# Third group of the first layer as four quadrant matmuls, with the conv stream and its turning moved around the inverses

## The chip, the cores and the metric

The kernel runs on one core of one Trainium2 chip. The time is device microseconds of that core from start to end of one execution, as the median of several runs.

## The reference

The input is an image batch of 4 x 48 x 128 x 128 (fp32). Two residual parts follow each other:

```python
x = x + conv_ref(ln_c(x))      # layer norm over channels; 3x3 conv on 12 of the 48 channels;
                               # 1x1 conv 48 -> 254; rfft2 on 8x8 patches, times fft_w, irfft2;
                               # gelu(a) * b on the two halves of 127; 1x1 conv 127 -> 48
t = tokens(x)
t = t + ffn_ref(ln_t(t))       # 48 -> 192 -> 48 with relu; inputs and weights rounded to fp8 e5m2,
x = from_tokens(t)             # sums and activations rounded to fp16
```

The first layer of the second part has 192 outputs: two times 128 rows hold the first 128 of them, and 64 are left. They are called the third group here.

## The kernel before

The work is cut into 32 steps, each a band of 16 image rows (two half bands j of 8 rows, 48 channels each, at partitions 0 and 64). It is a pipeline over seven steps: in step t the x of band t is transposed, the conv of band t-2 is made, the mix (1x1 conv) and the patch transforms of band t-3 and the end of those of t-4, the first layer of band t-5 and the second layer of band t-6. `live(t, d)` says whether band t-d exists, `at(t, d)` is its number. The loops run t = 0 to 34 (`run`), then comes a drain written out by hand. The program is unrolled. Every engine has its own `step(t)` with a hand-written order, and the engines meet by semaphores only, so an engine's order of work and its waits set the schedule. There is no planner.

What TensorE does in a step (lines 761 to 883): transposes of x into banks 0 and 1 (L784), the forward transform or coefficients (L803), inverse 3 of the band before (L532 its first half, L539 its second), mixes 0 and 1 (L519), projection (L548), second layer (L632, L639), inverse 0, turn of the tokens (L653), turn of the row statistics (`rows`, L613), turn of the rest (L663), mix 2. Then comes the part that is changed: first layer groups 0 and 1 of half c = 0 (`hidden`, L619), first half of inverse 1, group 2 of c = 0 (in `last_group`), second half of inverse 1, the conv `stream` (L568) into bank 3, mix 3, groups 0, 1 and 2 of c = 1, the turning of the conv (`convolve`, L577, from the copy `convs` back into bank 3), inverse 2. In steps 3 to 5 the row statistics are turned in `last_group`, from step 6 on earlier in the step, behind the turn of the tokens.

Groups 0 and 1 use 48 rows each (0 to 47 and 64 to 111) and all 128 columns, one per half band. Group 2 uses both half bands at once: rows 0 to 111, with weights `l1h[:, 2]` that are block diagonal. Each group's 512 columns are the tokens of half c. ScalarE copies them to `hid16` (`accumulators`, L897), VectorE adds the bias and cuts at zero (`relu`, L1276), and one step later ScalarE converts to `hid8` (`activations`, L906) for `second_layer`.

Other operations that are spoken of: ScalarE's gelu (L889) behind the first half of each inverse, its copy of the stream to `convs` (L1114) and its read of the turned conv into `zpix` (L1122, semaphore `conv_read`), `rows` (L913, the copy of the turned statistics to `rm_t`), and `convert` in the drain (L985). VectorE's `gate` (L1245), `weigh` (L1234) and `low_parts` (L1222, `zl`). The row statistics go from `rm_t` by SP's DMAs to `rm_scratch` (L403) and back to `crm` (L415), GpSimd makes the normalised conv channels from them (L1513 to L1521), SP stores these (L308) and loads the nine shifted `taps` (L333, L335), which the stream reads.

Steps with t below 8 or from 24 on are called peeled. In them TensorE waits at the top for everything of the step before:

```python
before = lambda behind: min(t[1] - behind, STEPS)
...
pe.wait_ge(conv_read, upto(before(2)))
...
pe.wait_ge(hid16_ready, upto(6 * before(5)))
```

In the others `conv_read` is waited for only ahead of the coefficients (L803).

## Time and profile before

| | us |
|---|---|
| runs | 699.67, 699.83, 700.46 |
| median of the runs | 699.83 |
| span of the profiled execution | 699.4 |

| engine | busy us | share |
|---|---|---|
| TensorE (PE) | 666.5 | 95% |
| its weight loads (PEld) | 529.3 | 76% |
| VectorE (DVE) | 597.9 | 85% |
| ScalarE (ACT) | 536.8 | 77% |
| GpSimd (POOL) | 456.9 | 65% |

All durations in the prediction are of the profiled execution; no own total besides its span is given for it. A busy share of 95% is an average over filling, steps and drain. Matmuls are pipelined: a matmul of 128 columns is shown with 0.27 us and the next starts 0.11 us later, so the start of one group and the start of the next say how long TensorE's array is taken.

### The profile page before, as it was taken

What the parts mean: (1) busy time and instruction counts of PE and PEld (TensorE: products, weight loads), DVE (VectorE), ACT (ScalarE), POOL (GpSimd) and SP (SyncE); (2) the same over time, 40 slices, a digit from 0 to 9 for tenths busy, and PEclk for the clock granted to TensorE, in tenths of its full rate; (3) what the DMA queues carried; (4) which work ended last, traced back from release to release, by engine and by line L of the source; (5) the groups of instructions that cost most, each with busy time, mean ns of one, the idle gap of its engine ahead of it and who ended that gap; (6) DMA issues with size and microseconds to landing.
All of it is one profiled execution on the core that took longest, in us unless ns stands there. A gap on an engine that the chain in (4) does not pass through costs nothing.

```text
span 699.4 us, 19176 instructions
## 1 busy us (share of the span) xinstructions
PE 666.5 (95%) x6620; PEld 529.3 (76%) x6620; DVE 597.9 (85%) x1159; ACT 536.8 (77%) x1087; POOL 456.9 (65%) x347
## 2 busy tenths in 40 slices
PE   4879999999999999999999999999999999999984
PEld 4657877778778877787878877787788777887751
DVE  7637889988988899988988899889888999877877
ACT  4244568888888888888889888888888888877784
POOL 2605677767777777677776877677777876753353
PEclk9989999999999999999999999999999999999995
DMA  4434445444544554445444544545445543342102
GB/s 102 79 78 118 121 113 131 112 126 128 142 120 118 142 140 121 114 120 138 127 123 131 139 131 107 132 121 144 121 116 144 139 129 103 100 119 87 47 23 68
DMA packets 52207, 80.73 MB, mean 115 GB/s; under 512 B 20823, under 2 KB 36079, under 8 KB 52111
## 3 DMA queue, kind: packets, MB, share of 16 engines
q1 hardware_dynamic: 50031, 78.56, 43.2%
q10 hardware_dynamic: 2080, 0.94, 0.6%
q8 instruction: 54, 0.88, 0.6%
q14 instruction: 42, 0.34, 0.2%
HBM read 63.17 MB, written 16.30 MB: 114 GB/s over the span
## 4 chain that ended last, share of the span: by engine, by line
PE 87%; DVE 3%; DMA 3%; issue 2%; ACT 1%; SPq 1%; POOL 1%; DVEq 0%; ACTq 0%; POOLq 0%
PE inva L532 17%; PE invb L539 15%; PE mixp L519 13%; PE misc L548 8%; PE misc L803 8%; PE misc L619 4%; PE misc L519 4%; PE misc L663 3%; PE misc L784 3%; PE misc L568 2%; PE misc L577 2%; PE misc L653 2%; PE mixp L632 2%; PE mixp L639 2%; DMA xin<-in_x_dram 1%
## 5 line engine op out<-in xcount | busy, mean ns | idle before, releaser
L1555 POOL TENSOR_TENSOR st<-st,neg_half 128x16 f32<-128x16 f32 x32 | 93.3, 2915 | 129.2 <-DVE st L1459 129.2
L532 PEld LDWEIGHTS inva<-inv,gmix 128*127 128x127 f32 x1024 | 123.4, 191 | 25.3 <-issue 16.6
L532 PE MATMUL inva<-inv,gmix 128*127 128x128 f32 x1024 | 141.0, 281 | 0.6 <-DVE gmix L1234 0.6
L1234 DVE TENSOR_TENSOR gmix<-mixp,freq_w 128x508 f32<-128x508 f32 x192 | 122.6, 680 | 16.9 <-PE mixp L519 16.9
L539 PE MATMUL invb<-inv,gmix 128*127 128x128 f32 x1024 | 134.7, 274 | 0.1
L539 PEld LDWEIGHTS invb<-inv,gmix 128*127 128x127 f32 x1024 | 126.2, 191 | 2.1 <-DVE hbuf L1245 0.5
L897 ACT ACTIVATE hid<-misc 128x512 f16<-128x512 f32 x180 | 94.1, 599 | 17.7 <-PE misc L619 17.7
L1245 DVE TENSOR_TENSOR hbuf<-gact,invb 127x512 f32<-127x512 f32 x128 | 87.4, 683 | 22.2 <-ACT gact L889 17.7
L1584 POOL TENSOR_TENSOR st<-st,neg_half 128x16 f32<-128x16 f32 x31 | 95.4, 3077 | 16.4 <-DVE st L1313 15.9
L906 ACT ACTIVATE hid<-hid 128x512 fp8e5<-128x512 f16 x174 | 93.2, 619 | 0.0
L889 ACT ACTIVATE gact<-inva 127x512 f32<-127x512 f32 x128 | 77.5, 605 | 19.9 <-PE inva L532 19.3
L519 PE MATMUL mixp<-win,zh 60*128 60x254 f16 x768 | 89.9, 272 | 0.7 <-DVE gmix L1234 0.6
L519 PE MATMUL mixp<-win,zl 60*128 60x254 f16 x768 | 89.0, 267 | 0.0
L1538 POOL TENSOR_TENSOR ob<-tch,y 112x1024 f32<-112x1024 f32 x29 | 62.1, 2140 | 34.1 <-DVE y L1294 34.1
L977 ACT ACTIVATE y<-mixp 112x512 f16<-112x512 f32 x58 | 31.4, 594 | 47.0 <-PE mixp L639 47.0
L803 PE MATMUL misc<-fwd,zpix 128*124 128x128 f32 x512 | 62.1, 275 | 0.0
L548 PE MATMUL misc<-hbuf,wout 127*64 127x512 f32 x248 | 60.1, 605 | 0.0
L803 PEld LDWEIGHTS misc<-fwd,zpix 128*124 128x124 f32 x512 | 58.6, 188 | 0.0
L519 PEld LDWEIGHTS mixp<-win,zh 60*128 60x128 f16 x768 | 37.1, 93 | 26.8 <-issue 14.5
L1435 DVE TENSOR_REDUCE st<-xpix 128x16 f32<-128x768 f32 x32 | 30.5, 952 | 28.3 <-ACT xpix L1068 28.3
L1580 POOL TENSOR_TENSOR tcen<-tpix,st 128x768 f32<-128x768 f32 x31 | 45.7, 1475 | 12.5 <-DVE st L1301 9.6
L1068 ACT ACTIVATE xpix<-misc 128x384 f32<-128x384 f32 x64 | 31.6, 494 | 23.2 <-PE misc L784 22.1
(184 smaller groups left out, 1358.2 us busy)
## 6 DMA issues: line engine op xcount, KB each, us to landing
taps<-cz_scratch SPq DMA_DIRECT2D x63, 292.2 KB
xin<-in_x_dram SPq DMA_DIRECT2D x64, 192.0 KB, 3.3
xres<-in_x_dram SPq DMA_DIRECT2D x64, 192.0 KB, 4.1
out_dram<-ob SPq DMA_DIRECT2D x60, 192.0 KB, 2.6
taps<-cz_scratch SPq DMA_DIRECT2D x63, 146.1 KB
crm<-rm_scratch SPq DMA_DIRECT2D x58, 96.0 KB
cx<-in_x_dram SPq DMA_DIRECT2D x32, 96.0 KB
cz_scratch<-cz SPq DMA_DIRECT2D x63, 48.8 KB
```

The costliest lines, as they stand in the source:

```text
L519: mm = pe.matmul(pair[q][:, e * HID2:(e + 1) * HID2], zpart[r0:r0 + KC, 2 * s + e, :], win[r0:r0 + KC, wpart, :], start=(e == 0 and zpart ...
L532: mm = pe.matmul(inva[0:HID, q * PX:(q + 1) * PX], gmix[:, s % 2, q, 0:HID], inv[:], start=True, stop=True, skip_group_check=True)
L539: mm = pe.matmul(invb[0:HID, q * PX:(q + 1) * PX], gmix[:, s % 2, q, HID:HID2], inv[:], start=True, stop=True, skip_group_check=True)
L548: mm = pe.matmul(dst[HALF * j:HALF * j + HALF, :], wout[:], hbuf[:, half, j, :, :], start=True, stop=True, skip_group_check=True)
L803: mm = pe.matmul(bank[(3, 0)[i // 4]][0:KSPAN, (i % 4) * PX:(i % 4 + 1) * PX], zpix[:, ring(t, 3), i, 0:KSPAN], fwd[:], start=True, stop=True,
L889: act.activation(gact[:, s % 2], inva[0:HID, :], ACT.Gelu).then_inc(gelu_ready, 1)
L897: act.activation(hid16[:, 3 * c + g, :], bank[g][:], ACT.Copy).then_inc(hid16_ready, 1)
L906: act.activation(hid8[:, 3 * c + g, :], hid16[:, 3 * c + g, :], ACT.Copy, saturate=False)\
L1234: dve.tensor_tensor(gmix[:, s % 2, 2 * q:2 * q + 2, 0:HID2], pair[q][:, 0:2 * HID2].rearrange("p (e c) -> p e c", e=2), freq_w[:], ALU.mul ...
L1245: dve.tensor_tensor(hbuf[:, s // 2, :, 2 * e:2 * e + 2, :], gact[:, s % 2].rearrange("p (j i c) -> p j i c", j=2, i=2), invb[0:HID, :].rea ...
L1555: pool.tensor_tensor(st1[:, 6, :], st1[:, 5, :], neg_half[:], ALU.pow).then_inc(pow1, 1)
L1584: pool.tensor_tensor(st2[:, 6, :], st2[:, 5, :], neg_half[:], ALU.pow).then_inc(pow2, 1)
```

## The change

Group 2 of both halves is made by `hidden_rest`: four matmuls of 48 rows by 64 columns, one for each pair of half band j and token half c. Half band j takes rows from 64 j on, token half c takes output partitions from 64 c on, and the result of half band j lies in bank 2 + j with both token halves one above the other. `hid16` and `hid8` have a new order of slots: 0 and 1 for c = 0, 2 (j = 1) and 3 (j = 0) for the rest, 4 and 5 for c = 1. The second layer reads slots 3 and 2 in `rest_product`, with as many matmuls as before.

TensorE's order from mix 2 on is now: groups 0 and 1 of c = 0, inverse 1 whole, `hidden_rest`, the row statistics (steps 3 to 5), mix 3, groups 0 and 1 of c = 1, stream, first half of inverse 2, the turning of the conv, second half of inverse 2. ScalarE's order is: copies 0 and 1, gelu 1, copies 2 and 3, rows (steps 3 to 5), copy 4, `convs`, copy 5, gelu 2, read of the conv. VectorE has three bias operations of two slots each. New waits: the stream and the early row statistics on copy 2, the second half of the transposes of x on copy 5 (in the steps that aren't peeled), `hidden_rest` on both squares `tsq`. In step 2 stream and turning stay together. In the drain the order of slots is followed, and the second layer inside inverse 3 waits for four conversions.

```diff
--- before.py
+++ after.py
@@ -560,6 +560,8 @@
                     pe.wait_ge(lo_ready, upto(2 * n + 2))
                 if live(t, 0):
                     pe.wait_ge(rmT_ready, a + 1 if a > 2 else 1)
+                if live(t, 5):
+                    pe.wait_ge(hid16_ready, 6 * at(t, 5) + 3)
                 pe.wait_ge(col_in, upto(64 * (c + 1)))
                 for turn in range(2):
                     rows = taps[:, turn].rearrange("p (r w) -> p r w", w=PW)
@@ -609,15 +611,34 @@
                 else:
                     pe.wait_ge(gmix_ready, upto(8 * n + 2))
                     pe.wait_ge(y16_ready, upto(2 * at(t, 6) + 2))
+                if live(t, 5) and a < ROWS_EARLY:
+                    pe.wait_ge(hid16_ready, 6 * at(t, 5) + 3)
                 dst = bank[3] if a < ROWS_EARLY else mixp[0]
                 pe.transpose(dst[0:32, 0:128], rm[:].rearrange("p a j i -> p (a j i)"), eye[:])\
                   .then_inc(rmT_done, 1)
 
+            def hidden_rest(t):
+
+                for c in range(2):
+                    for j in (1, 0):
+                        r0 = HALF * j
+                        mm = pe.matmul(bank[2 + j][HALF * c:HALF * c + HALF, :], l1h[r0:r0 + CH, 2, r0:r0 + HALF],
+                                       q16[r0:r0 + CH, 4 * c:4 * c + 4, :], start=True, stop=True,
+                                       skip_group_check=True)
+                        if c == 1:
+                            mm.then_inc(hid_done, 1)
+
             def hidden(t, c, g, dst):
 
                 r0, r1 = ((0, CH), (HALF, SPAN), (0, SPAN))[g]
                 pe.matmul(dst[:], l1h[r0:r1, g, :], q16[r0:r1, 4 * c:4 * c + 4, :], start=True, stop=True,
                           skip_group_check=True).then_inc(hid_done, 1)
+
+            def rest_product(dst, c, j):
+
+                r0, o = HALF * c, HALF * j
+                return pe.matmul(dst[o:o + HALF, :], l2[:, 2, r0:r0 + HALF], hid8[:, (3, 2)[j], :],
+                                 start=False, stop=True, skip_group_check=True)
 
             def second_layer(t):
 
@@ -627,17 +648,16 @@
                 pe.wait_ge(hid8_ready, upto(6 * l + 5))
                 pe.sem_inc(pe_held, 1)
                 for c in range(2):
-                    for g in range(2):
-                        r0 = HALF * g
-                        pe.matmul(pair[c][r0:r0 + HALF, :], l2[:, g, r0:r0 + HALF], hid8[:, 3 * c + g, :],
-                                  start=True, stop=False, skip_group_check=True)
-                for c in range(2):
                     if c == 1:
                         pe.wait_ge(hid8_ready, upto(6 * l + 6))
                         pe.sem_inc(pe_held, 1)
-                    for r0 in (0, HALF):
-                        mm = pe.matmul(pair[c][r0:r0 + HALF, :], l2[:, 2, r0:r0 + HALF], hid8[:, 3 * c + 2, :],
-                                       start=False, stop=True, skip_group_check=True)
+                    for g in range(2):
+                        r0 = HALF * g
+                        pe.matmul(pair[c][r0:r0 + HALF, :], l2[:, g, r0:r0 + HALF], hid8[:, 4 * c + g, :],
+                                  start=True, stop=False, skip_group_check=True)
+                for c in range(2):
+                    for j in range(2):
+                        mm = rest_product(pair[c], c, j)
                     mm.then_inc(y_done, 1)
 
             def turn_tokens(t):
@@ -691,6 +711,15 @@
                     for g in range(3):
                         hidden(t, c, g, dst[g])
 
+                def older_half(c, dst):
+                    for g in range(2):
+                        r0 = HALF * g
+                        pe.matmul(dst[r0:r0 + HALF, :], l2[:, g, r0:r0 + HALF], hid8[:, 4 * c + g, :],
+                                  start=True, stop=False, skip_group_check=True)
+                    for j in range(2):
+                        mm = rest_product(dst, c, j)
+                    mm.then_inc(y_done, 1)
+
                 def second_layer_half(c, dst):
                     for g in range(2):
                         r0 = HALF * g
@@ -704,11 +733,12 @@
                 t = (0, DRAIN)
                 pe.wait_ge(lo_ready, 2 * STEPS)
                 pe.wait_ge(h_ready, 4 * NEW + 2)
+                pe.wait_ge(hid16_ready, 6 * OLDER + 3)
                 project_half(0, bank[3])
 
                 def between():
-                    pe.wait_ge(hid8_ready, 6 * OLDER + 3)
-                    second_layer_half(0, mixp[0])
+                    pe.wait_ge(hid8_ready, 6 * OLDER + 4)
+                    older_half(0, mixp[0])
 
                 inverse(t, 4, 3, between)
                 pe.wait_ge(hid16_ready, 6 * OLD)
@@ -720,7 +750,7 @@
                 project_half(1, mixp[1])
                 pe.wait_ge(hid8_ready, 6 * OLD)
                 pe.wait_ge(y16_ready, 2 * OLDER + 1)
-                second_layer_half(1, mixp[0])
+                older_half(1, mixp[0])
                 pe.wait_ge(tpix_ready, 2 * NEW + 1)
                 pe.wait_ge(tsq_ready, 2 * NEW + 1)
                 first_layer(OLD, 0, (bank[0], bank[2], invb))
@@ -781,6 +811,8 @@
                         pe.wait_ge(eye_in, 16)
                     pe.wait_ge(xord_ready, upto(a + 1))
                     for i in range(PAIRS):
+                        if i == 4 and not peeled:
+                            pe.wait_ge(hid16_ready, upto(6 * l + 6))
                         mm = pe.transpose(bank[i // 4][:, (i % 4) * 128:(i % 4) * 128 + XSPAN],
                                           xord[:, i * PX:(i + 1) * PX], eye[0:XSPAN, 0:XSPAN])
                         if i % 4 == 3:
@@ -844,37 +876,29 @@
                     hidden(t, 0, 0, bank[0])
                     hidden(t, 0, 1, bank[1])
 
-                def last_group():
-                    if live(t, 0) and 3 <= a < ROWS_EARLY:
-                        rows(t, 0)
-                    if live(t, 5):
-                        pe.wait_ge(tsq_ready, upto(2 * m + 1, 2 * STEPS))
-                        hidden(t, 0, 2, bank[2])
-
-                if live(t, 3):
-                    inverse(t, 3, 1, last_group)
-                else:
-                    last_group()
+                if live(t, 3):
+                    inverse(t, 3, 1)
+                if live(t, 5):
+                    pe.wait_ge(tsq_ready, upto(2 * m + 2, 2 * STEPS))
+                    hidden_rest(t)
+                if live(t, 0) and 3 <= a < ROWS_EARLY:
+                    rows(t, 0)
                 if a == 2:
                     keep_busy(16, bank[1])
-                if live(t, 2):
-                    stream(t)
-                    if peeled and a == 2:
-                        keep_busy(2, bank[1])
                 if live(t, 3):
                     mix(t, 3)
                 if live(t, 5):
                     pe.wait_ge(hid16_ready, upto(6 * k + 2))
                     hidden(t, 1, 0, bank[0])
                     hidden(t, 1, 1, bank[1])
-                    pe.wait_ge(hid16_ready, upto(6 * k + 3))
-                    hidden(t, 1, 2, bank[2])
                 if live(t, 2):
-                    convolve(t)
+                    stream(t)
                     if peeled and a == 2:
+                        keep_busy(2, bank[1])
+                        convolve(t)
                         spread(2)
                 if live(t, 3):
-                    inverse(t, 3, 2)
+                    inverse(t, 3, 2, (lambda: convolve(t)) if live(t, 2) else None)
 
             run(pe, step)
             drain()
@@ -888,22 +912,22 @@
                 act.wait_ge(h_ready, upto(4 * n + s - 1))
                 act.activation(gact[:, s % 2], inva[0:HID, :], ACT.Gelu).then_inc(gelu_ready, 1)
 
-            def accumulators(t, c, groups):
+            def accumulators(t, groups):
 
                 k = at(t, 5)
                 for g in groups:
-                    act.wait_ge(hid_done, upto(6 * k + 3 * c + g + 1))
-                    act.wait_ge(hid8_ready, upto(6 * (k - 1) + 3 * c + g + 1))
-                    act.activation(hid16[:, 3 * c + g, :], bank[g][:], ACT.Copy).then_inc(hid16_ready, 1)
-
-            def activations(k, c, groups):
+                    act.wait_ge(hid_done, upto(6 * k + g + 1))
+                    act.wait_ge(hid8_ready, upto(6 * (k - 1) + g + 1))
+                    act.activation(hid16[:, g, :], bank[(0, 1, 3, 2, 0, 1)[g]][:], ACT.Copy).then_inc(hid16_ready, 1)
+
+            def activations(k, groups):
 
                 for g in groups:
-                    act.wait_ge(relu_ready, upto(6 * k + 3 * c + g + 1))
-                    if c == 0 and g == 0:
+                    act.wait_ge(relu_ready, upto(6 * k + g + 1))
+                    if g == 0:
                         act.wait_ge(y_done, upto(2 * k))
                     act.sem_inc(act_held, 1)
-                    act.activation(hid8[:, 3 * c + g, :], hid16[:, 3 * c + g, :], ACT.Copy, saturate=False)\
+                    act.activation(hid8[:, g, :], hid16[:, g, :], ACT.Copy, saturate=False)\
                        .then_inc(hid8_ready, 1)
 
             def rows(t, behind):
@@ -981,7 +1005,7 @@
 
                 def convert(k, c, g, tile=None):
                     act.wait_ge(relu_ready, 6 * k + 3 * c + g + 1)
-                    act.wait_ge(y_done, 2 * (k - 1) + c + 1)
+                    act.wait_ge(y_done, 2 * (k - 1) + (c + 1 if k == NEW else 2))
                     act.activation(hid8[:, 3 * c + g, :], hid16[:, 3 * c + g, :], ACT.Copy, saturate=False)\
                        .then_inc(hid8_ready, 1)
 
@@ -1086,8 +1110,7 @@
                 if live(t, 4):
                     gelu(t, 4, 3)
                 if live(t, 6):
-                    activations(l, 0, range(3))
-                    activations(l, 1, range(3))
+                    activations(l, range(6))
                 if live(t, 6):
                     sums(t, range(2))
                 if live(t, -1):
@@ -1101,27 +1124,29 @@
                 if live(t, 4):
                     rest(t)
                 if live(t, 5):
-                    accumulators(t, 0, (0,))
+                    accumulators(t, (0, 1))
+                if live(t, 3):
+                    gelu(t, 3, 1)
+                if live(t, 5):
+                    accumulators(t, (2, 3))
                 if live(t, 0) and 3 <= a < ROWS_EARLY:
                     rows(t, 0)
                 if live(t, 5):
-                    accumulators(t, 0, (1, 2))
-                if live(t, 3):
-                    gelu(t, 3, 1)
+                    accumulators(t, (4,))
                 if live(t, 2):
                     c = at(t, 2)
                     act.wait_ge(stream_done, upto(c + 1))
                     act.activation(convs[:].rearrange("p u x -> p (u x)"), bank[3][:], ACT.Copy)\
                        .then_inc(convs_ready, 1)
                 if live(t, 5):
-                    accumulators(t, 1, range(3))
+                    accumulators(t, (5,))
+                if live(t, 3):
+                    gelu(t, 3, 2)
                 if live(t, 2):
                     act.wait_ge(conv_done, upto(c + 1))
                     dst = halves(zpix[:, ring(t, 2)])[:, :, 0:2 * CC].rearrange("p (g u) c -> p g u c", u=4)
                     src = bank[3][:].rearrange("p (u g c) -> p g u c", u=4, g=4)[:, :, :, 0:2 * CC]
                     act.activation(dst, src, ACT.Copy, scale=1.0 / SCALE).then_inc(conv_read, 1)
-                if live(t, 3):
-                    gelu(t, 3, 2)
 
             def setup():
                 act.wait_ge(zeroed, 1)
@@ -1267,14 +1292,12 @@
                 order = lambda i: st1s[:, ring(t, behind, 8), i, :].rearrange("p (i j) -> p j i", j=2)
                 dve.tensor_tensor(rm[:, 1], order(6), order(2), ALU.mult).then_inc(mr_ready, 1)
 
-            def relu(t, c, parts=((0, 2), (2, 1))):
+            def relu(t, i):
 
                 k = at(t, 5)
-                for g, size in parts:
-                    dve.wait_ge(hid16_ready, upto(6 * k + 3 * c + g + size))
-                    buf = hid16[:, 3 * c + g:3 * c + g + size, :]
-                    dve.tensor_scalar(buf, buf, bq[:, g // 2:g // 2 + 1], 0.0, ALU.add, ALU.max)\
-                       .then_inc(relu_ready, size)
+                dve.wait_ge(hid16_ready, upto(6 * k + 2 * i + 2))
+                buf = hid16[:, 2 * i:2 * i + 2, :]
+                dve.tensor_scalar(buf, buf, bq[:, i % 2:i % 2 + 1], 0.0, ALU.add, ALU.max).then_inc(relu_ready, 2)
 
             def scale_tokens(t):
 
@@ -1372,7 +1395,7 @@
 
                 def convert(k, c, g):
                     dve.wait_ge(relu_ready, 6 * k + 3 * c + g + 1)
-                    dve.wait_ge(y_done, 2 * (k - 1) + c + 1)
+                    dve.wait_ge(y_done, 2 * (k - 1) + (2 if k == OLD else c + 1))
                     dve.tensor_copy(hid8[:, 3 * c + g, :], hid16[:, 3 * c + g, :], saturate=False).then_inc(late_hid8, 1)
 
                 def bias_half(l, c, buf):
@@ -1492,6 +1515,7 @@
                     weigh(t, 3)
                 if live(t, 5):
                     relu(t, 1)
+                    relu(t, 2)
                 if live(t, 3):
                     gate(t, 3, 2)
                 if isinstance(a, int) and a == 4:
```

## Rows read from the trace of the kernel before

**Rows 1.** The page: busy time, and the chain that ended last.

```profile
PE 666.5 (95%) x6620; PEld 529.3 (76%) x6620; DVE 597.9 (85%) x1159; ACT 536.8 (77%) x1087; POOL 456.9 (65%) x347
...
PE 87%; DVE 3%; DMA 3%; issue 2%; ACT 1%; SPq 1%; POOL 1%; DVEq 0%; ACTq 0%; POOLq 0%
```

**Rows 2.** Waits of TensorE, the longest: us in total, times, longest.

```profile
PE misc L784 <- ACT xord L934: 9.4, 2, 7.3
```

**Rows 3.** Timeline of TensorE, a steady step: start, us, operation.

```profile
371.17 0.38 PE L619 MATMUL misc<-q,l1h 48*128 48x512 f16 x2
...
371.48 1.15 PE L532 MATMUL inva<-inv,gmix 128*127 128x128 f32 x8
...
372.47 0.38 PE L619 MATMUL misc<-q,l1h 112*128 112x512 f16 x1
...
372.69 1.05 PE L539 MATMUL invb<-inv,gmix 128*127 128x128 f32 x8
...
373.67 0.65 PE L568 MATMUL misc<-taps,wpc 108*32 108x512 f16 x8
...
374.25 0.28 PE L519 MATMUL mixp<-win,zh 60*128 60x254 f16 x2
...
375.13 0.70 PE L619 MATMUL misc<-q,l1h 48*128 48x512 f16 x3
...
375.67 0.60 PE L577 MATMUL misc<-eye,convs 128*128 128x128 f32 x4
...
376.11 1.05 PE L532 MATMUL inva<-inv,gmix 128*127 128x128 f32 x8
...
376.99 1.05 PE L539 MATMUL invb<-inv,gmix 128*127 128x128 f32 x8
...
377.77 0.75 PEld L784 LDWEIGHTS misc<-eye,xord 96*128 96x128 f32 x8
377.88 0.82 PE L784 MATMUL misc<-eye,xord 96*128 96x96 f32 x8
```

**Rows 4.** Timeline of ScalarE, the same step.

```profile
371.97 0.48 ACT L967 ACTIVATE tsq<-misc 128x384 f32<-128x384 f32 x1
372.33 1.55 ACT L897 ACTIVATE hid<-misc 128x512 f16<-128x512 f32 x3
373.76 0.60 ACT L889 ACTIVATE gact<-inva 127x512 f32<-127x512 f32 x1
374.37 0.60 ACT L1114 ACTIVATE convs<-misc 128x512 f32<-128x512 f32 x1
```

**Rows 5.** Timeline at a peeled step's entry (t = 26): ScalarE, then TensorE.

```profile
495.67 0.51 ACT L1122 ACTIVATE zpix<-misc 128x384 f32<-128x384 f32 x1
...
496.56 0.83 PE L784 MATMUL misc<-eye,xord 96*128 96x96 f32 x8
```

**Rows 6.** Timeline where a mix waits for VectorE (t = 5).

```profile
84.44 1.27 DVE L1222 TENSOR_TENSOR zl<-misc,zh 124x512 f16<-124x512 f32 x2
...
85.77 0.28 PE L519 MATMUL mixp<-win,zh 60*128 60x254 f16 x2
```

**Rows 7.** Timeline of steps 3 and 4: row statistics, channels, taps, stream.

```profile
57.03 0.27 PE L613 MATMUL misc<-eye,rm 128*32 128x128 f32 x1
...
64.03 0.73 POOL L1513 TENSOR_TENSOR cz<-cx,crm 96x256 f32<-96x256 f32 x1 [4.88 <-issue]
...
70.52 0.78 SPq L333 DMA_DIRECT2D taps<-cz_scratch  x1
...
75.49 1.05 PE L539 MATMUL invb<-inv,gmix 128*127 128x128 f32 x8
...
77.50 0.65 PE L568 MATMUL misc<-taps,wpc 108*32 108x512 f16 x8 [0.96 <-DMA taps<-cz_scratch]
```

**Rows 8.** Timeline of the drain: conversions, and the second layer inside inverse 3.

```profile
671.53 2.21 ACT L985 ACTIVATE hid<-hid 128x512 fp8e5<-128x512 f16 x4
...
673.92 0.41 PE L697 MATMUL mixp<-hid,l 128*64 128x512 fp8e5 x2
```

## Prediction

> **What bounds the kernel now.** First the page: TensorE is busy 95% of the span, and the chain that ended last lies on it for 87% [rows 1]. Then its waits: the longest in total is 9.4 us for the ordered x at the very start, and no wait repeats from step to step [rows 2]. Then the timeline of one steady step: blocks follow each other without a gap, so a step is the sum of TensorE's blocks [rows 3]. Its length is 19.78 us: the transposes of x start at 377.88 and, six steps on, at 496.56 [rows 3, 5]. So I count in starts: a block lasts until the next one starts. Busy time would mislead, for matmuls overlap at their ends.
>
> What the reader should see in [rows 3] is the price of a change of the array's shape. The inverses and turns use the whole array, the mix and the first two groups of the first layer two halves of 64 rows side by side, the conv stream four strips of 32 columns. One wave of 512 columns costs 0.22 us with no change (372.47 to 372.69). The pair at 371.17 is one wave too, but takes 0.31 until the inverse: 0.10 for the change. The inverse behind it takes 0.99 where the one at 376.11 takes 0.88: 0.11 more. The inverse ahead of the stream takes 0.98: 0.10. Stream 0.58, two waves of 0.22 and 0.14 around the change to the mix. Mix, then pair, same shape: 0.88, no change. Pair and third group 0.54: two waves and 0.10.
>
> **The change, part by part.**
>
> *Steady step, TensorE.* Before, from the pair at 371.17 to the transposes at 377.88: 0.31 + 0.99 + 0.22 + 0.98 + 0.58 + 0.88 + 0.54 + 0.44 + 0.88 + 0.89 = 6.71 us [rows 3]. Two third groups over the whole array (0.22 each) become four matmuls of 48 rows by 64 columns, each in its own quadrant, with row halves writing different banks. No row shows four quadrants at once; bounds are 0.22 (all four together, as the stream's four strips go) and 0.43 (two at a time). I take 0.22, because halves by rows and strips by columns each run side by side in [rows 3]. After: pair 0.31, inverse 1 0.99 + 0.98 (0.10 for the change to quadrants), quadrants 0.22 + 0.10, mix 0.88, pair 0.22 + 0.10 (to the stream's strips), stream 0.58, first half of inverse 2 0.99 (now behind strips), turning 0.44, second half 0.89. Sum 6.70; in whole, one wave is saved (0.22) and two extra changes with one slow inverse start are bought (0.10 + 0.11). Rounded rows leave -0.01 to -0.05; I take -0.03. The 30 steps with a first layer (t = 5 to 34): **-0.9 us**. A change from quadrants to halves by rows is in no row; it could be free (-0.10 a step, -3 us) or as dear as strips to halves (0.14, +1 us).
>
> The Trainium skill ("TensorEngine Tiling (Array Packing)", Key Properties) says that changing the tiling mode, not just the tile, drains the array; the trace agrees, with 0.10 us at each change. It speaks against this change: by it the saved wave is paid back, and without it the step would be 0.2 us shorter.
>
> *The other engines in a steady step.* ScalarE gets the same six copies of 0.48 (from 372.33 to 373.76 for three), gelu and convs of 0.60 [rows 4], reordered. Against the new TensorE times: two copies to 373.3, gelu 1, then two copies to 374.9 (the quadrants end near 373.8), fifth copy at 375.1, convs at 375.6 (the stream ends near 375.6) to 376.2, sixth copy, gelu 2 at 376.7, read of the conv at 377.3. The turning may load its weights near 376.4: the convs lead by 0.1. What hides everything is only that 0.1; if it goes, each step stalls. The added waits (stream and turn of x on copies three and six, quadrants on the second squares, which end at 372.45) are met by the same times, with nothing queued behind them late. VectorE has three bias operations in place of four and waits for nothing new; the taps get 1.3 us more time, so SP's loads gain slack. Cost: nothing. GpSimd's queue is not touched in these steps.
>
> *Entry of the peeled steps.* This is the term that decides. In steps outside 8 to 23 TensorE waits at the top, before the transposes, until the conv of the step before has been read (line 775). Before, ScalarE read it ahead of gelu 2: from 495.67 to 496.18, 0.38 before the transposes at 496.56 [rows 5]. Now the turning lies inside inverse 2 and the read behind gelu 2. Counted back from the transposes at T: second half from T-0.89, turning from T-1.33; the first half's last matmul ends 0.17 later (376.11 + 1.05 against 376.99), T-1.16. Then gelu 2 from T-1.12, 0.60; the read from T-0.52, 0.51: it ends at T-0.01. From an engine's end to TensorE's next start is 0.06 (zl ends at 85.71, the mix starts at 85.77) [rows 6], and one more wait stands in between, some 0.06 by the same row. But the transposes' weights want to be loaded 0.11 ahead (377.77 for 377.88) [rows 3]. Stall: between 0.1 (a first matmul that needs no lead) and 0.3 (the sixth copy late by 0.1); I take **0.20**. It hits entries 4 to 7 and 24 to 34: 15 x 0.20 = **+3.0 us**. Steady steps wait for it only at the coefficients, 0.66 later, which covers it.
>
> *Filling, t = 3 to 5.* The turn of the row statistics moves from between the halves of inverse 1 to behind it. At t = 3 it lay in a wait for a gate; now its 0.11 stands alone, with 0.05 of extra changes: **+0.15**. It starts at 58.4 and not 57.03: 1.38 later. SP, GpSimd and SP again hang on it in a row (GpSimd starts at 64.03 behind 4.9 us of waiting, taps are issued from 70.52), and these are the taps that step 4 waits for, at 77.50 where 75.49 + 0.98 = 76.47 would do: a stall of 1.03 [rows 7]. The stream goes 0.98 later by its new place, the taps land 1.38 later, and the step is 0.35 late already: stall 1.0 again, **0**. Were the taps not tied to the rows, the stall would all but vanish: -0.9. At t = 5 the turn must wait until ScalarE has copied the quadrant result out of bank 3: 0.38 + 0.04 + 0.60 + 0.06 = 1.08 behind the quadrants' start instead of 0.3, [rows 3, 4, 6]: **+0.8**. Later steps turn the rows elsewhere.
>
> *Drain.* It now waits for four conversions and not three before the second layer inside inverse 3; four end at 673.74, the layer starts at 673.92 [rows 8]. Nothing, down to a cover of 0.1.
>
> Sum: -0.9 + 3.0 + 0.15 + 0 + 0.8 = +3.05 us on the profiled execution's 699.4, so 702.45. The runs' median of 699.83 lies 0.4 above that span: **702.9 us**.
>
> **Rivals.**
>
> *The quadrants pay (faster).* If changes to and from quadrants and from strips to the inverse are free or overlapped, the step is 0.20 shorter in place of 0.03: 30 x 0.20 = -6.0, +3.95 for entries and filling: 699.83 - 2.05 = 697.8. The point is at 0.13 a step: above it the saving beats the 3.95. For it: no row shows quadrants. Against it: every change of shape in [rows 3] costs 0.10 or more.
>
> *No entry stalls (within the noise or faster).* If ScalarE's read is not what the entry waits for, 3.0 falls away: 699.9. Or if half the changes are free, 702.9 - 3 = 699.9 too. Against it: line 775 and the 0.38 of lead that is given up.
>
> *The quadrants go two by two (change doesn't do what it says).* The step grows by 0.21 more: 702.9 + 6.4 = 709.3. Against it: halves by rows and by columns both run side by side.
>
> *ScalarE becomes late at the turning.* Its lead is 0.1; were the convs 0.1 late beyond that, 28 steps x 0.1 = +2.8: 705.7.
>
> **Numbers.** Forecast 0.60; quadrants pay 0.17; no entry stall or half the changes free 0.13; two by two 0.05; ScalarE late 0.05. The forecast's own range, from 0.1 to 0.3 at the entries and -0.05 to +0.01 a step, is 701.0 to 704.5. To leave out no more than 2 in 10 I reach to 698.0 and 705.5. A measurement can tell 0.2% (1.4 us) from no change. Below 698.4: 0.19. Within: 0.15. Above 701.2: 0.66.
>
> **What would show it.** Right: steady steps of 19.75 us; four L619-like matmuls with starts a few ns apart and 0.3 us to the mix; inverse 2's first half 0.99; a new wait of the transposes for the conv read in steps 4 to 7 and 24 to 34, making them 0.2 longer than the middle ones; at t = 5 a wait of 0.8 at the row turn; stall at t = 4 still near 1.0. Wrong: steady steps of 19.6 or below, or of 19.95; peeled steps as long as middle ones; a stall ahead of the turning.

## The result, and the profile after

The change takes 703.49 us in the median (701.86 to 706.32); the kernel before, run beside it, 700.25 us. The ratio is 1.0047, with a 95% interval of 1.0032 to 1.0062: 3.3 us slower, between 2.2 and 4.3. One of the change's eight executions was slow, 3335 us: it is left out of the range, the ratio and the interval, but not of the 703.49 (703.12 without it), and its cause isn't known. The forecast was 702.9 us where before stood at 699.83, so +3.05.

The profiled execution had 702.74 us and a span of 700.6. The page of the changed kernel: busy time, then the chain that ended last (to hold against [rows 1]), then its longest waits of TensorE ([rows 2]; us in total, times, longest).

```profile
PE 666.4 (95%) x6680; PEld 526.4 (75%) x6680; DVE 593.5 (85%) x1129; ACT 542.7 (77%) x1087; POOL 456.8 (65%) x347
...
PE 86%; DVE 3%; issue 3%; DMA 2%; ACT 1%; POOL 1%; SPq 1%; DVEq 0%; ACTq 0%; POOLq 0%
```

```profile
PE misc L816 <- ACT xord L958: 9.4, 2, 7.3
...
PE misc L617 <- ACT hid L921: 0.8, 1, 0.8
```

The totals tell nothing: TensorE is as busy as before, and the new waits are single ones. The answer is in the length of the steps. A step is counted here from its first coefficient matmul to that of the next step, in us, from each kernel's trace, so it ends with the entry of the next one; "rows" are the row statistics, and e1 to e10 are the experiments further down.

| step | before | change | rows back (e2) | rows back, no entry wait (e7) | before, rows late (e5) | before, turning inside (e8) | stream ahead (e4) | stream ahead, step 4 as changed (e9) |
|---|---|---|---|---|---|---|---|---|
| 3 | 16.71 | 16.76 | 16.76 | 16.74 | 17.31 | 16.65 | 16.52 | 16.72 |
| 4 | 18.99 | 19.77 | 18.07 | 17.99 | 22.48 | 19.45 | 19.41 | 18.28 |
| 5 | 19.64 | 20.66 | 19.72 | 19.63 | 20.26 | 19.98 | 19.59 | 19.58 |
| 6 | 19.78 | 20.44 | 19.86 | 19.77 | 19.78 | 20.12 | 19.73 | 19.75 |
| 8 to 22, each | 19.780 | 19.767 | 19.767 | 19.767 | 19.780 | 19.773 | 19.727 | 19.727 |
| 24 to 29, each | 19.78 | 19.86 | 19.86 | 19.77 | 19.78 | 20.12 | 19.73 | 19.73 |
| 32 and 33, each | 18.99 | 19.16 | 19.16 | 19.16 | 18.99 | 19.42 | 18.93 | 18.93 |

From step 3's coefficients to the end the change takes 656.3 us (a span of 700.56, less 44.24), the kernel before 653.1 (699.39 less 46.28). That is 3.2 more, close to the 3.3 of the ratio. The spans themselves differ by 1.2 only, because step 3 starts 2.0 us earlier in the change's profile. That isn't the change's doing: this start lies between 43.8 and 46.3 us over all the profiles, and at 45.9 in the second profile of the change (a1). What differs there between the two is the granted clock: 0.50 from 39.8 to 46.7 us in the kernel before, from 39.8 to 43.2 in the change. The same stretch of both, before and then the change (busy time of each engine, then PEclk, DMA share, GB/s):

```profile
44.00:45.00 1.00, 1.00 (x3) 0.52 (x3) 0.00 (x0) 0.00 (x0) 0.00 (x0) 0.50 0.00 0
```

```profile
44.00:45.00 1.00, 1.00 (x12) 1.00 (x11) 0.82 (x3) 0.89 (x3) 0.00 (x0) 1.00 0.00 0
```

By my estimate 3.4 us more at half the clock are up to 1.7 of the 2.0 us. The start is left out of what follows.

**A middle step** of the change, the timeline of TensorE, against [rows 3]:

```profile
371.49 0.38 PE L634 MATMUL misc<-q,l1h 48*128 48x512 f16 x2
371.80 1.15 PE L532 MATMUL inva<-inv,gmix 128*127 128x128 f32 x8
372.79 1.05 PE L539 MATMUL invb<-inv,gmix 128*127 128x128 f32 x8
373.77 0.41 PE L625 MATMUL misc<-q,l1h 48*64 48x512 f16 x4
374.11 0.28 PE L519 MATMUL mixp<-win,zh 60*128 60x254 f16 x2
...
374.99 0.38 PE L634 MATMUL misc<-q,l1h 48*128 48x512 f16 x2
375.30 0.65 PE L570 MATMUL misc<-taps,wpc 108*32 108x512 f16 x8
375.88 1.15 PE L532 MATMUL inva<-inv,gmix 128*127 128x128 f32 x8
376.87 0.60 PE L579 MATMUL misc<-eye,convs 128*128 128x128 f32 x4
377.30 1.05 PE L539 MATMUL invb<-inv,gmix 128*127 128x128 f32 x8
378.19 0.74 PE L816 MATMUL misc<-eye,xord 96*128 96x96 f32 x7
```

The four quadrant matmuls are one group of 0.41 us, hardly longer than the pair's 0.38: they run side by side. But 0.34 passes from their start (373.77) to the mix (374.11), 0.21 for the wave (512 columns streamed through once) and 0.13 for the change of shape. The stream's place gives 0.31 ahead of it, and inverse 2's first half takes 0.99 behind it. From the pair to the transposes: 6.70 us, before 6.71.

**The entry of a peeled step**, ScalarE and then TensorE (t = 27), against [rows 5]:

```profile
515.71 0.60 ACT L913 ACTIVATE gact<-inva 127x512 f32<-127x512 f32 x1
516.21 0.48 ACT L1149 ACTIVATE zpix<-misc 128x384 f32<-128x384 f32 x1
```

```profile
515.95 1.05 PE L539 MATMUL invb<-inv,gmix 128*127 128x128 f32 x8
516.90 0.77 PE L816 MATMUL misc<-eye,xord 96*128 96x96 f32 x7
```

The second half of the inverse takes 0.95 until the transposes where it takes 0.89 in the middle step, and the transposes take 0.69 until the coefficients where they take 0.66: 0.09 in all. The read ends at 516.69 and the transposes start 0.21 later.

**Step 4**, TensorE at the stream, against [rows 7]:

```profile
74.25 0.27 PE L617 MATMUL misc<-eye,rm 128*32 128x128 f32 x1
...
75.23 0.27 PE L519 MATMUL mixp<-win,zl 60*128 60x254 f16 x2
77.14 0.65 PE L570 MATMUL misc<-taps,wpc 108*32 108x512 f16 x8 [1.64 <-DMA taps<-cz_scratch]
```

The mix now stands ahead of the stream, and still TensorE waits 1.7 us for the taps, not 1.0. In step 3 the rows are turned at 56.19, which is 20.95 before this stream; in the kernel before it was 57.03 to 77.50, 20.47.

**Step 5**, TensorE, and the ScalarE copy that it waits for:

```profile
95.21 0.41 PE L625 MATMUL misc<-q,l1h 48*64 48x512 f16 x4
96.40 0.27 PE L617 MATMUL misc<-eye,rm 128*32 128x128 f32 x1 [0.79 <-ACT hid L921]
```

```profile
95.66 1.08 ACT L921 ACTIVATE hid<-misc 128x512 f16<-128x512 f32 x2 [0.64 <-PE misc L625]
```

**Step 6**, TensorE's projection and second layer, in the kernel before:

```profile
107.11 1.94 PE L548 MATMUL misc<-hbuf,wout 127*64 127x512 f32 x8
108.88 0.60 PE L632 MATMUL mixp<-hid,l 128*64 128x512 fp8e5 x4
```

and in the change, then VectorE and GpSimd:

```profile
106.93 1.94 PE L548 MATMUL misc<-hbuf,wout 127*64 127x512 f32 x8
109.10 0.62 PE L656 MATMUL mixp<-hid,l 128*64 128x512 fp8e5 x4 [0.24 <-DVE gmix L1259]
```

```profile
106.71 0.30 DVE L1475 SCALAR_TENSOR_TENSOR st<-st 128x16 f32<-128x16 f32 x1
107.05 0.17 DVE L1478 SCALAR_TENSOR_TENSOR st<-st 128x16 f32<-128x16 f32 x1
107.26 0.52 DVE L1482 TENSOR_SCALAR st<-st 128x16 f32<-128x16 f32 x1
107.69 1.27 DVE L1259 TENSOR_TENSOR gmix<-mixp,freq_w 128x508 f32<-128x508 f32 x2
```

```profile
106.59 0.40 POOL L1543 CAST cz<-cz 96x256 f16<-96x256 f32 x1 [0.19 <-POOL cz L1539]
107.07 0.68 POOL L1545 TENSOR_TENSOR cz<-cz 96x256 f16<-96x256 f32 x1
```

VectorE's first and third short operation, 0.17 us each elsewhere, last until GpSimd's operation is over: to 107.01 behind 106.99, and to 107.78 behind 107.75. So `weigh` starts late, and TensorE's second layer 0.41 us late: 2.17 us behind the start of the projection, 1.77 in the kernel before. The same pattern stands in a second profile of the change (a1: 0.32 and 0.52 us).

### The profile page after: what moved, and what is told of

Read it like the earlier page. It is cut to its first block, busy times and chain, and to the rows that moved or that the text cites. A ratio compares the mean times of both kernels' runs of the same rounds, so it can differ in the third digit from the quotient of the medians.

```text
span 700.6 us, 19299 instructions
## 1 busy us (share of the span) xinstructions
PE 666.4 (95%) x6680; PEld 526.4 (75%) x6680; DVE 593.5 (85%) x1129; ACT 542.7 (77%) x1087; POOL 456.8 (65%) x347
## 4 chain that ended last, share of the span: by engine, by line
PE 86%; DVE 3%; issue 3%; DMA 2%; ACT 1%; POOL 1%; SPq 1%; DVEq 0%; ACTq 0%; POOLq 0%
PE inva L532 18%; PE invb L539 15%; PE mixp L519 13%; PE misc L835 8%; PE misc L548 8%; PE misc L519 4%; PE misc L683 3%; PE misc L816 3%; PE misc L570 2%; PE misc L579 2%; PE misc L634 2%; PE mixp L656 2%; PE misc L673 2%; PE mixp L640 2%; PE misc L625 1%
## 5 line engine op out<-in xcount | busy, mean ns | idle before, releaser
L532 PE MATMUL inva<-inv,gmix 128*127 128x128 f32 x1024 | 144.2, 284 | 0.6 <-DVE gmix L1259 0.6
L539 PEld LDWEIGHTS invb<-inv,gmix 128*127 128x127 f32 x1024 | 123.7, 191 | 1.1 <-DVE hbuf L1270 0.7
L921 ACT ACTIVATE hid<-misc 128x512 f16<-128x512 f32 x180 | 100.5, 596 | 5.8 <-PE misc L625 1.6
```

The costliest lines, as they stand in the source:

```text
L532: mm = pe.matmul(inva[0:HID, q * PX:(q + 1) * PX], gmix[:, s % 2, q, 0:HID], inv[:], start=True, stop=True, skip_group_check=True)
L539: mm = pe.matmul(invb[0:HID, q * PX:(q + 1) * PX], gmix[:, s % 2, q, HID:HID2], inv[:], start=True, stop=True, skip_group_check=True)
L921: act.activation(hid16[:, g, :], bank[(0, 1, 3, 2, 0, 1)[g]][:], ACT.Copy).then_inc(hid16_ready, 1)
```

## The experiments

Each was run beside the kernel before on one chip; ratios are to that kernel, with their 95% interval.

**e1, no entry wait** (in `step` of TensorE):

```diff
-                    pe.wait_ge(conv_read, upto(before(2)))
+                    if t[1] < 4:
+                        pe.wait_ge(conv_read, upto(before(2)))
```

> The changed kernel without TensorE's wait for the conv read at the entry of the peeled steps 4 to 34 (it still waits for it ahead of the coefficients, as the middle steps do). Theory 1 (the entry wait is what makes the peeled steps longer): steps 24 to 31 fall from 19.86 us to the middle steps' 19.77, the gap ahead of the transposes from 0.17 to 0.11 us; steps 32 to 34, which begin with the coefficients, keep their 0.11 more. Entries 4 to 7 and 24 to 31 together give back 12 x 0.09 = 1.1 us, so about 702.4 where the change has 703.5. Rival (something else in the peeled steps, as their other waits): 19.86 stays and nothing is gained.

Ratio 1.0022 (1.0008 to 1.0035). Steps 24 to 29 fall to 19.767 us, steps 32 and 33 stay at 19.16. The timeline of TensorE at the entry of step 26:

```profile
495.71 0.82 PE L817 MATMUL misc<-eye,xord 96*128 96x96 f32 x8
```

ScalarE's read ends at 495.57 here, 0.14 ahead of the transposes, and nothing stops. The wait is the whole extra length of the peeled steps' entries up to 31; at 32 to 34 the coefficients come first and need the read itself. The median, 702.32 us, meets the expected 702.4, but not by these entries alone. Step 6 is 20.13 us here and not 20.44: the turn of step 5 waits as in the change, yet GpSimd starts its four operations on the channels 7.45 us behind it and not 8.46, is done by 106.06, and VectorE's last short operation is a normal one:

```profile
105.41 0.65 POOL L1546 TENSOR_TENSOR cz<-cz 96x256 f16<-96x256 f32 x1
```

```profile
106.35 0.17 DVE L1483 TENSOR_SCALAR st<-st 128x16 f32<-128x16 f32 x1
```

TensorE's second layer comes 1.77 us behind the projection again. What is left over in step 6, 0.36 us, is a wait for the taps.

**e2, rows back between the halves of inverse 1** (steps 3 to 5; ScalarE's copy ahead of gelu 1):

```diff
-                    inverse(t, 3, 1)
+                    inverse(t, 3, 1, (lambda: rows(t, 0)) if early_rows else None)
...
+                    if early_rows:
+                        pe.wait_ge(rmT_ready, a + 1)
                     hidden_rest(t)
-                if live(t, 0) and 3 <= a < ROWS_EARLY:
-                    rows(t, 0)
```

> The changed kernel with the turn of the row statistics of steps 3 to 5 put back between the halves of inverse 1 (ScalarE's copy of them ahead of gelu 1). Theory 1 (these statistics feed GpSimd, the channels and the taps, and at step 5 they wait for ScalarE's copy of bank 3): TensorE's wait of about 0.9 us at step 5 goes, the stall for the taps at step 4 falls from 1.9 by 0.9 to 1.4 us, and the 0.41 us at the second layer of step 6 goes, because GpSimd's four operations on the channels start before VectorE's statistics again and VectorE's last one takes 0.17 us and not 0.52. Together 2.0 to 2.9 us less: 700.6 to 701.5. Rival (the late GpSimd has nothing to do with step 6): the 0.41 stays.

Ratio 0.9992 (0.9981 to 1.0003), 700.03 us: the change without its loss, and more was won than expected, since the stall of step 4 went wholly. Step 4 takes 18.07 (the stream follows the mix without a wait: rows at 55.34, stream at 75.97, 20.63 apart), step 5 19.72, step 6 19.86, of which 0.09 is the entry wait. VectorE's short operations in step 6 are normal again, as GpSimd has finished by 102.94:

```profile
104.59 0.17 DVE L1474 SCALAR_TENSOR_TENSOR st<-st 128x16 f32<-128x16 f32 x1
...
105.00 0.17 DVE L1481 TENSOR_SCALAR st<-st 128x16 f32<-128x16 f32 x1
```

**e10, rows back in step 5 alone:**

```diff
-                    inverse(t, 3, 1)
+                    inverse(t, 3, 1, (lambda: rows(t, 0)) if t[1] == 5 else None)
...
-                if live(t, 0) and 3 <= a < ROWS_EARLY:
+                if live(t, 0) and t[1] in (3, 4):
                     rows(t, 0)
```

> The changed kernel with the row statistics between the halves of inverse 1 in step 5 alone (steps 3 and 4 as changed). It parts the two things that moving the rows did. Theory 1: TensorE's wait of 0.87 us at the turn of step 5 goes, and with it step 6's two stalls (0.41 at the second layer, 0.15 to 0.36 for the taps): step 5 about 19.8, step 6 about 19.86; step 4 keeps its stall for the taps of 1.6 to 1.8 us and stays near 19.7. In all -1.4 us against the change. Rival (the late statistics of steps 3 and 4 are what makes step 6 long): step 6 stays above 20.1.

Step 5 takes 19.72 and step 6 19.86: both extra lengths hang on the turn of step 5, not on steps 3 and 4. Step 4 stays long at 19.02, its stall 0.96 us in this profile (1.2 in the second one of the change, 1.7 in the first): how late the taps are differs between executions. The time, 702.07 us with a ratio of 1.0039 (1.0018 to 1.0060), is too wide to resolve 1.4 us: two of its eight runs took 706.2 and 706.8 us, at a mean granted clock of 0.977 and 0.975 where the other six have 0.981 to 0.984.

**e7, both repairs** (e2 with the edit of e1):

```diff
+                    if t[1] < 4:
+                        pe.wait_ge(conv_read, upto(before(2)))
```

> The changed kernel with both repairs, the row statistics of steps 3 to 5 between the halves of inverse 1 and no wait for the conv read at the entries. If the two costs are independent, this is the run with the rows alone less 12 x 0.09 = 1.1 us, 699 us, a ratio to the kernel before of 0.997 to 0.998; what is left of the change is then -0.013 us in each middle step, the stall for the taps that is gone at step 4, and 0.17 us in each of steps 32 to 34. Rival (they share a cause): same time as with the rows alone.

Ratio 0.9987 (0.9976 to 0.9999), 699.70 us. In the steps the two costs add up: 19.77 in step 6 and 19.77 in 24 to 29, and 1.0 us less than in e2 from step 3 to the end. The expected 0.997 to 0.998 lies a little below the ratio, within its interval.

**e3, third group over the whole array, order kept:**

```diff
-                for c in range(2):
-                    for j in (1, 0):
...
+                for c in range(2):
+                    hidden(t, c, 2, bank[3 - c])
...
+                return pe.matmul(dst[o:o + HALF, :], l2[:, 2, o:o + HALF], hid8[:, 2 + c, :],
```

> The changed kernel, its order kept, with the third group as two matmuls over the whole array (112 rows by 128 columns, one per token half) where the four quadrant matmuls stand. Theory 1 (the quadrants save a wave of 0.21 us and pay 0.09 for the change into their shape): steady steps get longer by 0.12 to 0.13 us, 19.89; 30 steps give +3.7 us, about 707. The reordering alone (stream behind the mix, turning inside inverse 2) then costs 0.11 a step against 19.78 of the kernel before. Rival (quadrants cost as much as they save): 19.77 stays.

Ratio 1.0062 (1.0047 to 1.0077), middle steps 19.860, so 705.7 us and not 707: the quadrants save less than the expected 0.12 to 0.13, and step 6 is 0.5 us shorter than in the change. The turn of step 5 waits here too, but GpSimd starts on the channels 7.09 us behind it, and the second layer isn't late. The quadrants save 0.093 us a step: a wave of 0.213 less 0.094 for the change into their shape, and less 0.03 because the mix behind them costs 0.13 and not 0.10. The new order alone costs 0.080 (19.860 - 19.780).

**e5, the kernel before with the rows late:**

```diff
-                    if live(t, 0) and 3 <= a < ROWS_EARLY:
-                        rows(t, 0)
...
+                if live(t, 0) and 3 <= a < ROWS_EARLY:
+                    rows(t, 0)
                 if a == 2:
```

> The kernel before with one part of the change alone: in steps 3 to 5 the row statistics are turned behind inverse 1 (ScalarE's copy behind gelu 1). Theory 1 (the taps of step 4 hang on the row statistics of step 3): TensorE's stall ahead of the stream of step 4 grows by 1.3 to 1.5 us and step 4 from 18.99 to about 20.3 us; no wait at step 5, since no quadrant result lies in bank 3, so step 5 stays at 19.64; GpSimd's channels come only about 1 us later in step 6 and miss VectorE's short operations, so step 6 stays at 19.78. In all +1.3 us. Rival (the taps' time is set by something else, as the stores or SP's other loads): step 4 grows by the turn's 0.11 only.

Ratio 1.0053 (1.0036 to 1.0069). The cause is confirmed, the size was missed: +3.7 us and not +1.3, and step 4 takes 22.48. The timeline of TensorE, then windows of 1 us (busy time of each engine, then PEclk, DMA share, GB/s):

```profile
76.61 0.27 PE L613 MATMUL misc<-eye,rm 128*32 128x128 f32 x1
79.73 0.65 PE L568 MATMUL misc<-taps,wpc 108*32 108x512 f16 x8 [2.85 <-DMA taps<-cz_scratch]
```

```profile
80.00:81.00 1.00, 1.00 (x18) 0.56 (x12) 0.00 (x0) 0.57 (x1) 1.00 (x1) 0.78 0.00 0
81.00:82.00 1.00, 1.00 (x11) 0.48 (x8) 0.00 (x0) 0.02 (x1) 0.25 (x1) 0.50 0.01 5
```

Without the mix ahead of it the stream waits 2.9 us, and then the granted clock falls to 0.50, its level of 1.2 GHz, for 3.4 us; the matmuls of the mix are 0.21 apart and not 0.11. Step 5 has a stall of 0.6 at the stream as well; step 6 is unharmed, as expected without the wait for bank 3.

**e8, the kernel before with the turning inside inverse 2, its read behind gelu 2:**

```diff
-                    inverse(t, 3, 2)
+                    inverse(t, 3, 2, (lambda: convolve(t)) if live(t, 2) else None)
...
+                if live(t, 3):
+                    gelu(t, 3, 2)
                 if live(t, 2):
                     act.wait_ge(conv_done, upto(c + 1))
```

> The kernel before with another part alone: the turning of the conv between the halves of inverse 2 and its read behind gelu 2. Theory 1: middle steps stay at 19.78 us (turning and inverse both use the whole array, no change of shape), entries of the peeled steps cost 0.09 each and steps 32 to 34 0.17 each: 12 x 0.09 + 3 x 0.17 = +1.6 us. Rival (the entry stall needs ScalarE's later copies, which only the change has): nothing.

Ratio 1.0058 (1.0035 to 1.0080), so 4 us and not 1.6. Middle steps 19.773, peeled ones 20.12. The timeline of ScalarE, then TensorE, at the entry of step 26:

```profile
495.32 1.57 ACT L897 ACTIVATE hid<-misc 128x512 f16<-128x512 f32 x3 [0.58 <-PE misc L619]
496.77 0.62 ACT L889 ACTIVATE gact<-inva 127x512 f32<-127x512 f32 x1
497.25 0.53 ACT L1124 ACTIVATE zpix<-misc 128x384 f32<-128x384 f32 x1
```

```profile
496.77 1.05 PE L539 MATMUL invb<-inv,gmix 128*127 128x128 f32 x8
497.98 0.69 PE L784 MATMUL misc<-eye,xord 96*128 96x96 f32 x6 [0.15 <-issue]
```

Three copies stand ahead of gelu 2 and the read here, in the change only one, so the read ends later and the entry costs 0.35 a step. By this reading the new places of its copies save the change most of this; no run moved the copies alone. My expectation missed it, since it took 0.09 over from a kernel with another order on ScalarE.

**e4, stream ahead of mix 3, turning ahead of inverse 2, read ahead of gelu 2** (e2, with the quadrants in banks 0 and 2, the later pair in banks 1 and 0):

```diff
-                        mm = pe.matmul(bank[2 + j][HALF * c:HALF * c + HALF, :], ...
+                        mm = pe.matmul(bank[(2, 0)[j]][HALF * c:HALF * c + HALF, :], ...
...
+                if live(t, 2):
+                    stream(t)
...
                 if live(t, 3):
                     mix(t, 3)
...
+                    hidden(t, 1, 0, bank[1])
+                    hidden(t, 1, 1, bank[0])
                 if live(t, 2):
-                    stream(t)
+                    convolve(t)
```

> Quadrant matmuls kept, the rest of the order as in the kernel before: rows of steps 3 to 5 between the halves of inverse 1, stream ahead of mix 3, turning ahead of inverse 2, conv read ahead of gelu 2; the quadrants write banks 0 and 2, the later pair banks 1 and 0. Theory 1 (each change of the array's shape costs 0.10 us, and an inverse behind a narrower shape 0.10 more; inverse 2 now starts behind a full-array turning): a steady step takes 19.78 - 0.21 (a wave) + 0.10 (inverse to quadrants, in place of inverse to stream: none) ... counted by changes, the kernel before has six in this part with the pair to inverse 1, this one has the same number: 19.57 to 19.67 us. Entries cost nothing. 30 steps x 0.11 to 0.21: 3.3 to 6.3 us below the kernel before, 694 to 697. Rival (the stream directly behind the quadrants, or the later pair waiting for ScalarE's copy of bank 0, opens a stall): 19.8 or more.

Ratio 0.9960 (0.9946 to 0.9975), 698.18 us: faster than both. But a step takes 19.727, not 19.57 to 19.67. Its timeline shows where the rest goes: 0.34 from the quadrants to the stream, 0.58 to the mix, 0.31 from the pair to the turning and 0.49 for that, 0.05 more than elsewhere.

```profile
372.40 0.41 PE L621 MATMUL misc<-q,l1h 48*64 48x512 f16 x4
372.74 0.65 PE L568 MATMUL misc<-taps,wpc 108*32 108x512 f16 x8
373.32 0.28 PE L519 MATMUL mixp<-win,zh 60*128 60x254 f16 x2
...
374.20 0.38 PE L630 MATMUL misc<-q,l1h 48*128 48x512 f16 x2
374.51 0.66 PE L577 MATMUL misc<-eye,convs 128*128 128x128 f32 x4
375.00 1.05 PE L532 MATMUL inva<-inv,gmix 128*127 128x128 f32 x8
```

**e6, e4 with the stream behind mix 3 in step 4:**

```diff
-                if live(t, 2):
+                if live(t, 2) and t[1] != 4:
                     stream(t)
...
+                if t[1] == 4:
+                    stream(t)
```

> The kernel with the stream ahead of mix 3 (the fastest so far), with the stream behind mix 3 and the later pair's place in step 4 alone, where TensorE waited 1.5 us for the taps. Theory 1 (the taps land at a time that TensorE's order does not move): mix 3's 0.88 us fills the wait, step 4 falls from 19.41 to 18.5 us, 697.3 us in all. Rival (the taps are later by as much, or the turning then waits for ScalarE): no gain.

Step 4 fell by 0.17 us only: 0.46 is still waited ahead of the stream, and the turning then waits for ScalarE's copy, as the rival had it. Ratio 0.9975 (0.9963 to 0.9988), no gain over e4.

```profile
77.62 0.65 PE L568 MATMUL misc<-taps,wpc 108*32 108x512 f16 x8 [0.46 <-DMA taps<-cz_scratch]
78.97 0.66 PE L577 MATMUL misc<-eye,convs 128*128 128x128 f32 x4 [0.70 <-ACT convs L1135]
```

**e9, e4 with step 4 wholly in the changed order** (e6, and):

```diff
-                    inverse(t, 3, 2)
+                    inverse(t, 3, 2, (lambda: convolve(t)) if t[1] == 4 else None)
...
+                if t[1] == 4:
+                    gelu(t, 3, 2)
```

> The kernel with the stream ahead of mix 3 (19.727 us a step), but step 4 wholly in the changed order: stream behind mix 3, turning inside inverse 2, gelu 2 ahead of the conv read. Theory 1: the first half of inverse 2 now fills the 0.8 us in which the turning waited for ScalarE's copy of the stream; step 4 falls from 19.41 us to 18.1 to 18.5 and step 5's entry costs 0.1: 697 us, ratio 0.994 to 0.996. Rival: the taps land later again and the stall returns ahead of the stream: 19.2 as in the half repair.

Step 4 takes 18.28 us, 1.1 less than in e4. The ratio is 0.9959 (0.9946 to 0.9972), 697.34 us: faster than both kernels again; from e4 it can't be told apart by the times, only by the step.

**a1, the change again**, beside e9 and e10, unedited:

> The change itself on the same chip as the two others, for a direct comparison: ratio to the kernel before of 1.0047 again, 3.3 us; middle steps of 19.767, late peeled steps of 19.86, steps 4 to 6 between 19.8 and 20.7 us as in the first profile.

Ratio 1.0047 (1.0032 to 1.0061), middle steps 19.767, step 5 20.66, step 6 20.66; step 4, at 19.31, is below the expected 19.8 to 20.7.

## Why the prediction was right

The side was right, and so were the two mechanisms that cost time, the read at the entries and the late row statistics. That the size came so close (+3.3 us against +3.05) was luck in part: the entries cost half of what I took, the filling more than double, and these two errors cancelled. The profiled execution that the sum was made for came out at 700.6 and not at 702.45, by its earlier start of step 3; from there on it is +3.2.

- *Steady step, -0.03 each, -0.9 us.* It is -0.013 (19.780 to 19.767), -0.4 us over 30 steps. The quadrants run side by side, so the rival "two by two" falls. The sum of the blocks, 6.70 for 6.71, was met as it stands; the -0.03 was an allowance for rounding. What was mis-sized inside it is the change of shape behind the quadrants: taken as 0.10, it is 0.13, and I had named 0.14 as its dear end. "The quadrants pay" falls with it: they do save 0.093 (e3), and the order around them costs 0.080.
- *Entry of the peeled steps, 15 x 0.20 = +3.0 us.* Confirmed by e1 as the mechanism (the wait stands at line 769, not 775), but double of what it is: 0.09 in 12 entries and 0.10, 0.17 and 0.17 at the three last, some +1.5 us. The failed term is the read's end, taken as T-0.01. It ends 0.15 before the time at which the transposes would have started: it starts 0.50 behind gelu 2 and not 0.60, and lasts 0.48 and not 0.51. The lag, on the other hand, is 0.21 and not 0.12. The 0.60 was gelu's duration; its successor can start before its end, which [rows 4] already showed for the copies.
- *Filling, +0.15 at step 3 and +0.8 at step 5.* The wait at step 5 is there: 1.19 from the quadrants to the rows, 0.88 over the 0.31 worked out. Step 3 is 0.05 longer, not 0.15.
- *Step 4, nothing.* This was wrong: the stall grew from 1.0 to 1.7 us (1.2 in the other profile), and the step from 18.99 to 19.77. That the taps hang on the row statistics of step 3 was right: in all thirteen profiles 20.2 to 21.6 us lie between them. I had let the two shifts cancel to the last tenth, while the chain itself varies by 0.4 us between the two profiles of the change (20.95 and 20.52); why it varies stays open.
- *Step 6, not seen.* I followed the late rows to the taps, where they cost 0.15 us (0.36 in a1), but not to what else GpSimd's late start runs into. It costs 0.41 at the second layer. e2 and e10 take both away. That GpSimd's operations are the cause is read from the coinciding ends and from e1 and e3: with the turn of step 5 as late as here, but GpSimd's operations 1.0 and 1.4 us earlier behind it, the 0.41 is gone. No experiment moved them alone on purpose, and why the chain to GpSimd took longer in the change's two profiles stays open.
- *ScalarE late at the turning.* It did not happen in the middle steps: convs end at 376.60 and the turning starts at 376.87. I had given them 0.1 of lead, it is 0.27. *Drain.* As taken, nothing: 45.86 us from step 34's coefficients to the end before, 45.71 in the change.

In sum, from step 3 to the end of the steps: steady -0.4 for -0.9, entries +1.5 for +3.0, filling +2.2 for +0.95. The rival "no entry stalls" falls with e1. Its price was taken as 3.0 us; it would have been 1.5.

## What to carry to other kernels

Where TensorE has no gaps, count its blocks from start to start, and count changes of the array's shape beside the waves: four quadrant matmuls in one wave, where two waves stood, saved 0.21 us a step, and the shapes and the order around them took all but 0.01 of it back. An order that is right in the steady steps must be checked against the filling and the peeled steps on their own, where the waits are others: here thirty steps gave 0.4 us, and the entries and the filling cost 3.7. And the best version came from keeping the new matmuls while putting back the order that the rest of the chain was built around.

## What the runs showed of the hardware

- Matmuls of four quadrants (48 rows by 64 columns) start within 0.01 us of each other and end as a group after 0.41 us, where a pair of row halves takes 0.38.
- A change of the array's shape costs between 0.09 and 0.13 us, depending on the two shapes: 0.09 from whole to quadrants, 0.13 from quadrants to row halves or to strips. An inverse behind another shape takes 0.10 more in itself (0.99 for 0.89). By the Trainium skill ("TensorEngine Tiling (Array Packing)", Key Properties) changing the mode drains the engine; the runs agree in that each change costs time, and can't show the draining itself. A change of the columns' tiling alone, 64 rows kept, is dear too (0.13).
- Short VectorE operations on SBUF were held until a GpSimd operation ended (0.17 became 0.30 and 0.52 us). The Trainium skill ("SBUF — State Buffer", Terms) says that the two engines share a pair of ports that one holds for a whole instruction while the other blocks; the ends in the trace, 0.02 and 0.03 us apart, agree, and so does e1, where GpSimd was done earlier and the last of them took 0.17.
- A wait of 2.9 us on TensorE was followed by 3.4 us at the lower clock (e5), one of 1.7 us in the change's profile was not.
- Seven runs of the change spread over 4.5 us (701.86 to 706.32), those of the kernel before beside them over 1.5 (699.55 to 701.04). The change isn't shown to be the more restless of the two: beside a1 it was 2.9 (702.44 to 705.37) against 2.8 (699.57 to 702.36). The stall of step 4 differs by 0.5 us between two profiles of the change, which is part of the spread; where the rest comes from stays open.
